# Convolution of a spectral unit: both parities of an image in one mixing product, banks and slots in a new order

## The reference, cut to what matters

```
for i, frac in enumerate((1, 2, 4, 8)):
    xi = x[:, :T // frac]
    si = _stu(xi, sigma, phi, M_u[i], M_phi_plus[i], M_phi_minus[i])
...
U_plus = jnp.fft.irfft(Vf[None, :, :, None] * Uf_p[:, :, None, :], n=n, axis=1)[:, :sl]
out = jnp.einsum('btkd,k,kde->bte', U_plus, s, Mpp)
out = out + jnp.einsum('btkd,k,kde->bte', U_minus, s, Mpm)
```

## Time and profile before

| | us |
|---|---|
| median of 3 runs | 10391.0 |
| lowest, highest | 10381.18, 10395.99 |
| profiled execution, its own time | 10387.62 |
| its span, first to last instruction | 10385.7 |
| first and last matmul start of the convolution | 4471.9, 6898.1 |
| PE busy in the whole span | 8379.6 |
| DVE busy in the whole span | 6946.5 |

### The profile page before, as it was taken

The page is one execution under the profiler, slowest core; times in us unless marked ns, Lnnn a source line. Parts: engine busy times, 40 slices in busy tenths (PEclk is TensorE's granted clock), DMA queues, the critical chain, the costliest instruction groups (busy, mean ns, idle before and its releaser), DMA issues. The chain is left out here.

```text
span 10385.7 us, 129266 instructions
## 1 busy us (share of the span) xinstructions
PE 8379.6 (81%) x40748; PEld 6067.1 (58%) x40748; DVE 6946.5 (67%) x9145; ACT 4443.7 (43%) x8493; POOL 4258.6 (41%) x2945
## 2 busy tenths in 40 slices
PE   4777777777777777599999999967849899896657
PEld 2444444434443444389999999966625555554445
DVE  6999899989998999644444444443247566643446
ACT  4666566656665666422222222222423444453331
POOL 3999599959995999421111111100000000000001
PEclk8999999999998999899999999988968999998668
DMA  4555355535553555200000000013120100103000
GB/s 130 162 162 162 110 162 160 163 109 164 160 162 110 161 163 162 82 18 10 14 12 15 10 15 12 10 58 80 70 100 19 33 15 19 23 7 132 20 21 18
DMA packets 332597, 835.13 MB, mean 80 GB/s; under 512 B 35796, under 2 KB 111832, under 8 KB 318654
## 3 DMA queue, kind: packets, MB, share of 16 engines
q1 hardware_dynamic: 331910, 826.64, 25.9%
HBM read 758.85 MB, written 39.08 MB: 77 GB/s over the span
## 5 line engine op out<-in xcount | busy, mean ns | idle before, releaser
L754 POOL TENSOR_TENSOR ss_work<-ss_dtu,ss_ringb 128x768 f32<-128x768 f32 x1536 | 2758.0, 1820 | 252.2 <-POOLq L59 248.8
L618 PE MATMUL ss_ps<-ss_work,ss_ident 128*128 128x512 f32 (+1 forms) x6144 | 2278.7, 517 | 448.5 <-POOL ss_work L764 329.6
L618 PEld LDWEIGHTS ss_ps<-ss_work,ss_ident 128*128 128x128 f32 x6144 | 1222.5, 203 | 1224.4 <-issue 879.4
L738 DVE TENSOR_TENSOR_SCAN ss_work<-ss_ps,ss_last,ss_work 128x768 f32<-128x768 f32 x1024 | 1810.2, 1800 | 98.3 <-issue 44.3
L671 ACT ACTIVATE ss_ps<-ss_dt,ss_a_neg 128x768 f32<-128x768 f32 x1536 | 1376.1, 896 | 272.9 <-DVE ss_work L738 254.5
L1234 ACT ACTIVATE stu_XT<-cv_ps 128x384 fp32r<-128x384 f32 x768 | 377.8, 492 | 1788.9 <-DVE cv_ps L1281 1361.4
L723 DVE TENSOR_TENSOR ss_work<-ss_work,ss_ps 128x1152 f32<-128x1152 f32 x768 | 1018.5, 1326 | 1.2 <-ACT ss_ps L679 1.2
L2295 DVE TENSOR_REDUCE at_top<-at_ps 128x1 f32<-128x384 f32 x1512 | 727.5, 546 | 400.5 <-PE at_ps L2213 400.5
L2276 ACT ACTIVATE at_probs<-at_ps 128x768 f32<-128x768 f32 x864 | 653.6, 808 | 657.3 <-PE at_ps L2232 656.4
L738 DVE TENSOR_TENSOR_SCAN ss_work<-ss_ps,ss_work 128x768 f32<-128x768 f32 x512 | 879.2, 1743 | 66.9 <-POOL ss_work L754 36.3
L1275 DVE TENSOR_TENSOR stu_XT<-cv_ps,stu_XT 128x384 fp32r<-128x384 f32 x768 | 428.2, 558 | 637.9 <-ACT stu_XT L1234 615.1
(11 more groups left out here) (561 smaller groups left out, 14919.1 us busy)
## 6 DMA issues: line engine op xcount, KB each, us to landing
ss_ringb<-scan_rows SPq DMA_DIRECT2D x768, 384.0 KB, 3.7
ss_ringc<-scan_rows SPq DMA_DIRECT2D x768, 384.0 KB, 3.8
c_w<-in_l_ffn_w SPq DMA_DIRECT2D x52, 1024.0 KB, 13.3
at_packs<-at_high SPq DMA_DIRECT2D x64, 288.0 KB, 5.4
c_w_last<-in_l_ffn_w SPq DMA_DIRECT2D x12, 1024.0 KB, 13.5
cv_raw<-in_l_ffn_phi_odd SPq DMA_DIRECT2D x16, 576.5 KB, 3.6
cv_raw<-in_l_ffn_phi_even SPq DMA_DIRECT2D x16, 576.0 KB, 4.2
at_packs<-at_qk SPq DMA_DIRECT2D x32, 288.0 KB, 5.5
```

Of the source, the lines that this page charges most:

```text
L618: return pe.matmul(acc[:, d * WIN + a:d * WIN + e], ident[:, :], weighed[:, t % DEEP, d, a:e], start=n == 0 and e - a == 512, stop=n == NS ...
L738: dve.tensor_tensor_scan(hid[:, t % DEEP, d, ::step], decay[d][:, ::step], drive[:, t % DEEP, d, ::step], start, ALU.mult, ALU.add).then_i ...
L754: pool.tensor_tensor(drive[:, t % DEEP, d, :], dtu[:, t // NST % 2, d, :], ringb[:, t % RING, :], ALU.mult).then_inc(s["driven"], 1)
```

## The change

A unit is now an image with both parities: `m` runs over 8 units of a filter (4 images of kind 0, 4 of kind 1), and the same products are issued for q = 0 and q = 1 one after the other. Banks 0 and 1 hold the shared product and then stretch 1 of the two parities, banks 2 and 3 stretch 0 and then stretch 2, and the mixing writes to banks 4 and 5 or 6 and 7 by turns.

In `mix`, one matmul takes the same piece of both parities where a stretch is cut into pieces: its moving operand is two runs, `CW` apart in SBUF, and its output lies packed in one bank. Stretch 2 isn't cut, and keeps one matmul for each parity and turn. So the columns of a unit's mixing are 288, 288 and 192 (9 matmuls), 384 and 384 (6), and 384 for each parity (6). The number of products, their shapes and their operands stay.

The order on PE in unit `m` is SHARED of both parities, mix 2 of unit m-1, FIRST of both, SECOND of both, mix 0 of unit m, THIRD of both, mix 1 of unit m. DVE's adds for a unit are three (stretch 0), two (stretch 1) and one of 768 columns (stretch 2); joins and lowers stay one for each parity and stretch. The halving of matrices and their sums move to other places between units.

```diff
+        SHARED, FIRST, SECOND, THIRD = 0, 2, 4, 6
+        def bank_of(c, q):
+            return q if c == 1 else 2 + q
+
+        def parts_of(m, c):
+            first = 4 + 2 * ((m + c) % 2)
+            cuts = pieces(c)
+            if len(cuts) == 1:
+                return [(first + q, 0, slice(q, q + 1), *cuts[0]) for q in range(2)]
+            at, placed = [0, 0], []
+            for n, (lo, hi, seg) in enumerate(cuts):
+                placed.append((first + n % 2, at[n % 2], slice(0, 2), lo, hi, seg))
+                at[n % 2] += 2 * (hi - lo)
+            return placed
...
-                    pe.wait_ge(s["kept"], at)
-                    pe.wait_ge(s["lowered"], at + NCW)
-                    pe.wait_ge(s["added"], at)
-                    for lo, hi, seg in pieces(c):
+                    pe.wait_ge(s["kept"], done)
+                    pe.wait_ge(s["lowered"], done + 2 * NCW)
+                    pe.wait_ge(s["added"], k * MIXES + (NCW * m + c + 1))
+                    slot = 2 * ((m + c) % 2)
+                    for bank, at, qs, lo, hi, seg in parts_of(m, c):
+                        nq = qs.stop - qs.start
+                        out = ps[:, bank, at:at + nq * (hi - lo)].rearrange("p (q n) -> p q n", q=nq)
                         for turn, (a, f) in enumerate(HI_LO):
-                            ins = pe.matmul(ps[:, 4 + c, lo:hi], (eff_high, eff_low)[a][:, kind, seg, :], (uk_high, uk_low)[f][:, (NCW * n + c) % SLOTS, lo:hi],
+                            ins = pe.matmul(out, (eff_high, eff_low)[a][:, kind, seg, :], (uk_high, uk_low)[f][:, slot + qs.start:slot + qs.stop, lo:hi],
                                             start=turn == 0, stop=turn == 2, skip_group_check=True)
...
+                    for m in range(UNITS):
+                        kind, b = m // B, m % B
...
+                        for q in range(2):
+                            pe.wait_ge(s["lowered"], last + (2 + q + 1))
+                            product(kind, q, q, lambda a, g, parity: (s_high, s_low)[a][:, b * NCW + g, parity, :], near, CW, False, True, True).then_inc(s["convolved"], 1)
+                        if m or before is not None:
+                            mix(k if m else before, m - 1 if m else UNITS - 1, 2)
+                        for q in range(2):
+                            pe.wait_ge(s["lowered"], last + (4 + q + 1))
+                            product(kind, q, 2 + q, of(b, 0), near, 0, True, True, True).then_inc(s["convolved"], 1)
+                        for q in range(2):
+                            pe.wait_ge(s["shared"], k * SHARES + (2 * m + q + 1))
+                            product(kind, q, q, of(b, 1), less, 2 * P, False, True, True).then_inc(s["convolved"], 1)
+                        mix(k, m, 0)
+                        for q in range(2):
+                            pe.wait_ge(s["lowered"], last + (2 * NCW + q + 1))
+                            product(kind, q, 2 + q, of(b, 0), far, 2 * P, False, True, False)
+                            product(kind, q, 2 + q, of(b, 2), near, 0, True, False, True).then_inc(s["convolved"], 1)
+                        mix(k, m, 1)
...
+                def add(k, m, c):
+                    dve.wait_ge(s["mixed"], k * MIXES + (NCW * m + c + 3))
...
+                        out = YT[:, :, base:base + CW]
+                        ins = dve.tensor_tensor(out, out, ps[:, parts[0][0]:parts[0][0] + 2, 0:CW], ALU.add)
+                    else:
+                        for bank, at, _, lo, hi, _ in parts:
+                            out = YT[:, :, base + lo:base + hi]
+                            ins = dve.tensor_tensor(out, out, ps[:, bank, at:at + 2 * (hi - lo)].rearrange("p (q n) -> p q n", q=2), ALU.add)
+                    ins.then_inc(s["added"], 1)
...
+                    for m in range(UNITS):
+                        late = (k, m - 1) if m else (before, UNITS - 1)
+                        if late[0] is not None:
+                            add(*late, 1)
+                            add(*late, 2)
+                        if m == 1:
+                            for step in range(2):
+                                halve_matrices(step, 1, k * MIXES + 2)
+                        for q in range(2):
+                            lower(k, m, 0, q)
+                        for q in range(2):
+                            join(k, m, 1, q)
+                            lower(k, m, 1, q)
+                        add(k, m, 0)
+                        for q in range(2):
+                            join(k, m, 2, q)
+                            lower(k, m, 2, q)
+                        if after is not None:
+                            for step in ((), (), (), (), (0,), (1, 2), (3, 4), ())[m]:
+                                sum_matrices(step, after)
+                            if m == UNITS - 1:
+                                for step in range(2):
+                                    halve_matrices(step, 0, k * MIXES + (2 + MIXES // 2))
```

More of the change, by code:

```diff
@@ L1082, in convolve @@
 def convolve(nc, w, u_high, u_low, s_high, s_low, spare, YT, wk):
-    PAIRS = [(b, q) for b in range(B) for q in range(2)]
-    PER = 2 * len(PAIRS)
+    UNITS = 2 * B
+    PRODUCTS, CHUNKS = 8 * UNITS, 2 * NCW * UNITS
+    MIXES, SHARES, JOINS = NCW * UNITS, 2 * UNITS, 4 * UNITS
     WIDE, APART = 2 * CW, 5 * P
-    SLOTS = 4
     HI_LO = ((0, 0), (0, 1), (1, 0))
@@ L1104, in convolve @@
         shared = sb("shared", [P, 2, CW])
-        uk_high, uk_low = spare[:, 0:SLOTS, :], spare[:, SLOTS:2 * SLOTS, :]
+        uk_high, uk_low = spare[:, 0:4, :], spare[:, 4:8, :]
         ps = ctx.enter_context(nc.psum_tensor("cv_ps", [P, 8, 512], F32))
@@ L1160, in _, with product @@
             def _(pe):
-                def product(n, bank, blocks, taps, first, narrow, start, stop):
-                    kind, b, q = unit(n)
+                def product(kind, q, bank, blocks, taps, first, narrow, start, stop):
                     parity, shift = ((q, 0), (1 - q, q))[kind]
@@ L1173, in of, with mix @@
                     return lambda a, g, parity: (u_high, u_low)[a][:, b * GB + NCW * c + g, parity, :]
-                def mix(k, n, c):
-                    kind = n // len(PAIRS)
-                    if n % len(PAIRS) == 0 and c == 0:
+                def mix(k, m, c):
+                    kind = m // B
+                    if m % B == 0 and c == 0:
                         pe.wait_ge(s["eff_ready"], k * 2 + (kind + 1))
-                    at = k * (NCW * PER) + (NCW * n + c + 1)
-                    pe.wait_ge(s["kept"], at)
-                    pe.wait_ge(s["lowered"], at + NCW)
-                    pe.wait_ge(s["added"], at)
-                    for lo, hi, seg in pieces(c):
+                    done = k * CHUNKS + (2 * NCW * m + 2 * c + 2)
+                    pe.wait_ge(s["kept"], done)
[5 more added lines that the diff above has]
+                        out = ps[:, bank, at:at + nq * (hi - lo)].rearrange("p (q n) -> p q n", q=nq)
                         for turn, (a, f) in enumerate(HI_LO):
-                            ins = pe.matmul(ps[:, 4 + c, lo:hi], (eff_high, eff_low)[a][:, kind, seg, :], (uk_high, uk_low)[f][:, (NCW * n + c) % SLOTS, lo:hi],
+                            ins = pe.matmul(out, (eff_high, eff_low)[a][:, kind, seg, :], (uk_high, uk_low)[f][:, slot + qs.start:slot + qs.stop, lo:hi],
                                             start=turn == 0, stop=turn == 2, skip_group_check=True)
@@ L1189, in body @@
                 def body(k, before):
-                    for n in range(PER):
-                        kind, b, q = unit(n)
-                        if n % len(PAIRS) == 0:
+                    for m in range(UNITS):
+                        kind, b = m // B, m % B
+                        if m % B == 0:
                             pe.wait_ge(ready[kind], k + 2)
[L1194 to L1209, removed]
@@ L1211, in _ @@
-                pe.sem_inc(s["convolved"], 4 * PER)
+                        last = k * CHUNKS + 2 * NCW * m
+                        for q in range(2):
[3 more added lines that the diff above has]
+                            mix(k if m else before, m - 1 if m else UNITS - 1, 2)
@@ L1212, in _ @@
+                        for q in range(2):
[3 more added lines that the diff above has]
+                        mix(k, m, 1)
+                pe.sem_inc(s["convolved"], PRODUCTS)
                 body(0, None)
@@ L1214, in _ @@
                     body(i + 1, i)
-                for c in range(NCW):
-                    mix(NK - 1, PER - 1, c)
+                mix(NK - 1, UNITS - 1, 2)
             @block.scalar
             def _(act):
-                act.sem_inc(s["shared"], 1)
                 with act.Fori(0, NK) as k:
[L1222 to L1227, removed]
-                        for c in range(NCW):
[L1229 to L1234, removed]
+                    for m in range(UNITS):
+                        made = k * PRODUCTS + (PRODUCTS + 8 * m)
```

(43 more changed lines are left out.)

6 lines of the change are left out of this document (5 added, 1 removed).

## The result

The changed kernel takes 10245.86 us (median, 10241.29 to 10252.34), the one before in the same comparison 10393.49 us. The ratio is 0.9862, 95% interval 0.9846 to 0.9877. The prediction was 10242 us in 10222 to 10288. The profiled execution took 10241.29 us, with a span of 10239.4 us.

A forecast was written before the change was run, and what follows sets the result against it. PE, busy 2411.55 of 2426.20 us in the convolution, bounds it by issuing 16128 matmuls. Mixing −150 us and the end +1 give −149: 10239 from the profiled execution, 10242 with the median 3.4 us higher; range 10222 to 10288.

The forecast's parts named there:

- The price of a short matmul: PE's mixing: matmuls below some 200 columns cost a fixed 0.112 us; merging saves 1.17 us a unit, 150 us.
- Rival C: PE's matmuls: time follows the columns, none is removed, so nothing is gained, 10391 us; chance 0.03.
- The 288s: Six merged mixing matmuls of 288 columns in a unit: 0.132 us each, with bounds of 0.117 and 0.1756.
- Two runs: Moving operand of merged mixing matmuls: reading it in two runs was taken to cost nothing extra.
- Rival D: Mixing matmuls: two-run operands are read slower, kernel 10502 us; chance 0.05 together with any wait above 1.17 us.
- The order: New order on PE: moved waits cost nothing, tightest slack 2.1 us before mix 2 in an ordinary unit.
- Rival B: PE waits before mix 2 or mix 0 for ACT and DVE chains; 0.5 us a unit gives 10306; chance 0.12.
- The sum: Whole kernel: −150 us from mixing and 1 us at the end make −149 us, 10242 us; chance 0.80.
- the shared products of kind 0: Among the convolution's product matmuls, same shapes and operands as before: change of nothing, 0.1756 us for each of 384 columns.
- the 14 gaps of the loop: PE lacks work 14 times, about once each turn of the filter loop, 14.5 us together; these were to stay.

The follow-up runs named there:

- e8: The changed kernel with the mixing product of stretch 0 alone issued once for each parity; convolution 2397.0 us, 116 more than the changed kernel.
- e3: The changed kernel with 2 x 48 columns in the second and third turn of each 288-column mixing matmul; convolution 2270.2 us, 10.7 less.
- e2: e1 with only 64 of 128 weight columns loaded in 20 of the 30 short mixing matmuls of a unit; convolution 2347.0 us, kernel 10308.12 us.
- e4: The changed kernel with the moving operand of the merged mixing products read as one run, same widths, wrong columns mixed; convolution 2280.2 us.
- e5: The changed kernel with an idle DVE reduction of 1600 columns before the low part of stretch 2, parity 1; convolution 2279.3 us.
- e6: The changed kernel with an idle DVE reduction of 3840 columns before the low part of stretch 2, parity 1; convolution 2423.9 us, kernel 10390.1 us.
- e7: The changed kernel with banks exchanged, products in 4 to 7 and mixing in 0 to 3; convolution 2281.7 us.
- e1: The changed kernel with each mixing product issued once for each parity again, order and banks as changed; 10416.72 us, 1.0024 of the kernel before.
- e9: The changed kernel with three filters in each turn of PE's loop, same instructions and order; 10235.25 us, 0.985 of the kernel before.

## Why the prediction was right

**The price of a short matmul.** 0.112 us, solved from one unit of 63 matmuls, gave 0.88 us for stretch 0 (e8: 0.88) and 0.29 for stretch 1 (0.23 and 0.29). e3 shows that columns below the knee are free (the knee is the number of columns from which a matmul costs more than its weight load), e2 that the price goes with the weight columns. Rival C, by columns, is out on e3 alone. The Trainium skill says in the section that the prediction weighed (TensorE: Matmul & The Clock Gate, Back-to-back issue gap) that the isolated spacing leaves out the weight load. e2 agrees: half the weight columns in 20 matmuls made a unit 0.76 us shorter.

**The 288s.** 0.133 for 0.132. The bounds (0.117 and 0.1756) were far wider than needed.

**Two runs.** Rival D is out: e4. L409 of the earlier trace rows was the right row to go by, L627 the wrong one.

**The order.** It was laid out with 2.1 us of slack before mix 2; e5 and e6 find 2.2. Rival B is out, and e6 puts the point from which the change gains nothing at a chain 3.4 us late, where the prediction's numbers give 2.1 + 1.17 = 3.3.

**The sum.** −149 us was predicted; it is −145.3 in the convolution and −147.6 between the medians. Two units before take 18.76 us in kind 0 and 18.83 in kind 1, one unit after 17.66 and 17.67, so a unit saves 1.10 and 1.16 us where 1.17 was laid out. 3 of the 4 us that are missing are the shared products of kind 0 (e7), which the prediction held at nothing for being the same products. The lengths themselves, laid out as 18.74 and 17.58, were both a little short.

**What was right by luck.** The prediction said that the 14 gaps of the loop stay, with no reason. e1 shows that they need not have: with the same order and short matmuls in mix 1 they grow to 2.07 us, and with the clock behind them that is 28 us in all. e8, whose mix 1 is the merged one, keeps them at 1.41. So they stayed because mix 1 was merged, which the prediction did not weigh. It isn't the very last matmuls that count: the last six before the turn last 0.52 us in the kernel before and 0.56 in e1 (from their starts), and the gaps are 1.31 and 2.07. The last 18 fit better. They last 2.63 us in the kernel before, 2.61 in the changed one, 1.90 in e1 and 1.73 in e2, and the gaps are 1.31, 1.31, 2.07 and 2.21, longer by about what the 18 are shorter. e8 has 2.61 and 1.41. That these matmuls cover a part of the turn is a reading made after the fact; the number 18 was picked for its fit, and no run tested it. Why the clock fell behind 11 of 14 gaps in e1 and 2 of 14 in e2 stays open.

## What to carry to other kernels

Where PE is the bound, price its matmuls from start to start over a whole period, and look for those below the knee (here 0.112/0.1756 × 384, about 245 columns with 128 columns of weights, an estimate from the two prices): each costs 0.112 us whatever its columns, and merging two of them saves where the wider one costs less than 0.224, as the 288s (0.133) and the 384s (0.176) do. A moving operand in two runs with adjoining elements cost nothing here (e4). Before a new order is taken, lay out each wait with the chain that feeds it; and look at what stands before a loop's turn: twelve short matmuls in place of six wide ones made the turn some 0.7 us dearer here (1.31 and 1.41 to 2.07).

## What the runs showed of the hardware

- With 128 columns of weights, fp32r matmuls of 96 to 192 moving columns follow each other at 0.112 us, those of 288 at 0.133, those of 384 at 0.176. With 64 weight columns in two of three, the 18 of mix 0 went from 1.94 to 1.37 us (e2).
- A turn of PE's loop costs 1.3 us from matmul to matmul in the kernel before and in the changed one, 2.07 in e1 and 2.21 in e2, where mix 1 is made of twelve short matmuls. With three filters in a turn, 10 of 14 gaps are gone (e9).
- The granted clock fell from 1.00 to 0.50 behind 11 of e1's 14 gaps (1.79 to 2.33 us) and behind 2 of e2's 14 (1.93 to 2.48 us). Behind gaps of up to 1.70 us it never did (the kernel before, the changed one, e8).
- The same 18 shared products of kind 0 take 3.23 us in the changed kernel and 3.18 in e1; in kind 1 they take 3.18 and 3.20. The cause is open.
